# Layer 0's last tile of pairs made half as high and stacked, the split groups dealt out anew, two relus moved

## The chip, the core and the metric

The kernel runs on one core of a Trainium2 chip. The metric is the device time in microseconds (us) of one launch.

## What is computed

A batch of 512 rows looks up 39 embedding tables of width 16. A compressed interaction network of three layers follows, and then a small MLP. Cut to what matters (B = 512, 39 fields, D = 16):

```
x0 = xk = e                                    # (B, 39, 16), gathered
for idx, (W, b) in enumerate(params):          # three layers of 128 outputs
    z = relu(einsum('bhd,bkd,hks->bsd', x0, xk, W) + b[None, :, None])
    if idx != 2:
        xk = z[:, :64, :]; direct.append(z[:, 64:, :])
    else:
        direct.append(z)
h = concatenate([sum(concatenate(direct, axis=1), axis=-1), dense_ctx], axis=1)
y = relu(relu(h @ W_top1 + b_top1) @ W_top2 + b_top2) @ W_top3
```

## The kernel before

The batch is cut into C = 16 pieces of 32 rows, so that a row of a tile has N = 32 x 16 = 512 elements. A *tile* is a set of up to 128 pairs (a field of x0 and a row of xk), one on each partition. VectorE multiplies the two factors (`multiply`, L404), and TensorE contracts the tile with 128 x 128 weights into PSUM. Layers 1 and 2 have 39 x 64 pairs: 19 full tiles and one of 64 partitions (T1 = 20). Layer 0 is symmetric. Its 780 pairs lie in T0 = 7 full tiles, whose factors are `x0_same` (one anchor field for each partition, copied by the runs in `ANCHORS`) and `x0_rep` (the fields in rotation, `field_of`).

Tiles go in *groups* of two. `KINDS` gives each group a letter:

- `w`, whole: fp32 matmuls on the product as it is (L516, two instructions for a tile).
- `p` and `d`, split: ScalarE rounds the product (`round_high`, L625), GpSimd (`p`) or VectorE (`d`) subtracts to get the low part (`low_part`, L280), and TensorE makes three fp32r matmuls for each tile (L522, L524, L527).
- `h`, the last group of layers 1 and 2: one whole tile (L507), then the tile of 64 partitions, whose high and low parts lie one above the other in `stacks`. ScalarE makes the high part (L619), VectorE the low part (L423), and TensorE one fp32r matmul of 128 rows (L509) and one of 64 (L510).

```
KINDS = {1: "pwppwpwddh", 0: "dwww", 2: "wdwpwpwpwh"}
BODY = L1_GROUPS + L0_GROUPS + L2_GROUPS
```

A body for piece c walks through the 24 groups of BODY in order: indices 0 to 9 are layer 1 of piece c, 10 to 13 are layer 0 of piece c+1 and 14 to 23 are layer 2 of piece c. Layer 0 of piece 0 goes ahead of all bodies, and the last body has no layer 0. Every engine has its own instruction stream in this order, bound by semaphores:

- VectorE makes the products into a ring of 8 groups. The pairs (0, 1) and (2, 3) are one instruction each (`PAIRED`). The lows of its `d` and `h` groups come two groups late (`LOW_LAG`), and those still open are made at the latest ahead of layer 2. Index 0 waits for xk0, index 14 for xk1. xk0 and xk1 are PSUM banks; `x0_same` and `x0_rep` are in SBUF.
- ScalarE rounds, and it runs the relus that write xk and the direct outputs: layer 2 of the piece before at index 4, layer 1 at index 12, layer 0 of the next piece at index 18, each ahead of that index's rounding.
- GpSimd makes its lows in order. At index 10 it issues the ten indirect DMAs of `gather(c + 2)` (L360).
- SyncE's queue writes the gathered piece to DRAM (L297), loads `x0_same` with one DMA for each run of `ANCHORS` (L306), and then `x0_rep` in four parts of tiles, 0 to 3, 4 to 7, 8 to 13 and 14 to 19, two DMAs for each (L315).

Rounded and low parts have a ring of three slots (`PART_RING`). A slot is free when TensorE has used what was in it.

Of the kernel before, what the change touches and what calls it, by code (L numbers as in the profile page):

```python
# [41 lines left out]
def pairs_of_layer0():  # L42

    found = {}
    for t in range(T0):
        for p in range(S):
# [6 lines left out]
PARTS = [(0, 4), (4, 8), (8, 14), (14, T1)]  # L53


def part_of(t):

    return next(q for q, (first, end) in enumerate(PARTS) if first <= t < end)


# [10 lines left out]
STACKED = "whole, its second tile split and stacked"  # L71
LETTER = {"w": WHOLE, "d": LOW_DVE, "p": LOW_POOL, "h": STACKED}
# [20 lines left out]
SPLIT = [i for i, g in enumerate(BODY) if g[4] in (LOW_DVE, LOW_POOL)]  # L93
STACKS = [i for i, g in enumerate(BODY) if g[4] == STACKED]

RING = 8
# [12 lines left out]
    "split": lambda g: g[4] in (LOW_DVE, LOW_POOL),  # L109
    "stacked": lambda g: g[4] == STACKED,  # L110
    LOW_DVE: lambda g: g[4] == LOW_DVE,
# [37 lines left out]
def dlrm_cin_kernel(nc, ids, base, tables, dense, w0a, w0b, b0, bx0, w1, b1, bx1, w2, b2,  # L149
# [6 lines left out]
    with ctx:  # L156
# [130 lines left out]
        def _(sp):  # L287
# [20 lines left out]
            def load_replicated(c, half, q):  # L308

                first, end = PARTS[q]  # L310
                for e in range(2):
                    src = x0_rows[bass.ds(c, 1), T1 * e + first:T1 * e + first + 1, :]
# [14 lines left out]
            load_same(1, 1)  # L327
            sp.wait_ge(w_copied, len(BODY))
            sp.wait_ge(w_stack_made, len(STACKS))
# [57 lines left out]
        def _(dve):  # L387
# [31 lines left out]
            def make_low(c, index):  # L419
                if index in STACKS:  # L420
                    dve.wait_ge(stack_rounded, count("stacked", c, index))
                    at = STACKS.index(index)
                    nc.vector.tensor_tensor(stacks[HALF:128, at, :], products[0:HALF, index % RING, 1, :],  # L423
                                            stacks[0:HALF, at, :].bitcast(fp32), ALU.subtract).then_inc(stack_low, 1)
                else:
                    low_part(dve, nc.vector, c, index)

            def body(c, indices):
                late = []
                for index in indices:  # L430
                    layer, t, n, _, kind = BODY[index]
                    if layer == 1:
                        if t == 0:
                            dve.wait_ge(xk0_ready, c + 1)
                        if t == PARTS[part_of(t)][0]:
                            dve.wait_ge(rep_loaded[part_of(t)], 32 * (c + 1))
                    if layer == 0:
                        if t == 0:
                            dve.wait_ge(same_loaded, 16 * len(ANCHORS) * (c + 2))
                        if t == PARTS[part_of(t)][0]:  # L440
                            dve.wait_ge(rep_loaded[part_of(t)], 32 * (c + 2))
                    if layer == 2 and t == 0:
# [25 lines left out]
            for n_taken, index in enumerate(WEIGHT_ORDER):  # L468
# [5 lines left out]
                if index in WHOLES:  # L474
                    nc.vector.tensor_copy(w_whole[0:p, WHOLES.index(index), 0:n, :],
                                          w_sb[layer][0:p, t:t + n, :]).then_inc(w_copied, 1)
                else:
                    at = SPLIT.index(index)
# [5 lines left out]
            for at, index in enumerate(STACKS):  # L484
                layer, t = BODY[index][:2]
                dve.wait_ge(w_stack_rounded, at + 1)
                nc.vector.tensor_tensor(w_stack_low[:, at, :], w_sb[layer][0:HALF, t + 1, :],  # L487
                                        w_stack_high[0:HALF, at, :].bitcast(fp32), ALU.subtract) \
# [9 lines left out]
        def _(pe):  # L498
            tiles = [T0, T1, T1]

            def contract(c, index):
                layer, t, n, partitions, kind = BODY[index]
                slot, out = index % RING, z[layer][:, :]
                if kind == STACKED:
                    at, stack = WHOLES.index(index), STACKS.index(index)
                    pe.wait_ge(made, count("all", c, index))
                    nc.tensor.matmul(out, w_whole[:, at, 0, :], products[:, slot, 0, :], start=False, stop=False)  # L507
                    pe.wait_ge(stack_low, count("stacked", c, index))
                    nc.tensor.matmul(out, w_stack_high[:, stack, :], stacks[:, stack, :], start=False, stop=False)  # L509
                    mm = nc.tensor.matmul(out, w_stack_low[:, stack, :], stacks[0:HALF, stack, :],  # L510
                                          start=False, stop=True)
                elif kind == WHOLE:
                    at = WHOLES.index(index)
                    pe.wait_ge(made, count("all", c, index))
                    for i, p in enumerate(partitions):
                        mm = nc.tensor.matmul(out, w_whole[0:p, at, i, :], products[0:p, slot, i, :],  # L516
                                              start=(t + i == 0), stop=(t + i == tiles[layer] - 1))
                else:
                    at, part = SPLIT.index(index), part_slot(index)
                    pe.wait_ge(rounded, count("split", c, index))  # L520
                    for i, p in enumerate(partitions):
                        nc.tensor.matmul(out, w_high[0:p, at, i, :], high[0:p, part, i, :],  # L522
                                         start=(t + i == 0), stop=False)
                        nc.tensor.matmul(out, w_low[0:p, at, i, :], high[0:p, part, i, :], start=False, stop=False)  # L524
                    pe.wait_ge(low_by[kind], count(kind, c, index))
                    for i, p in enumerate(partitions):
                        mm = nc.tensor.matmul(out, w_high[0:p, at, i, :], low[0:p, part, i, :],  # L527
                                              start=False, stop=(t + i == tiles[layer] - 1))
                mm.then_inc(used, 1)

            def body(c, indices):
                first = isinstance(c, int) and c == 0
                for index in indices:
                    layer, t = BODY[index][:2]
                    if t == 0 and layer == 0 and not (isinstance(c, int) and c < 0):
                        pe.wait_ge(direct0_ready, c + 1)
                    if t == 0 and layer == 1 and not first:
                        pe.wait_ge(direct1_ready, c)
                    if t == 0 and layer == 2 and not first:
# [4 lines left out]
            pe.wait_ge(w_copied, len(BODY))  # L544
            pe.wait_ge(w_stack_made, len(STACKS))
# [49 lines left out]
        def _(act):  # L595
# [15 lines left out]
            def round_high(c, index):  # L611

                _, _, n, (p, *_), _ = BODY[index]
                if index in STACKS:
                    at = STACKS.index(index)
                    if not (isinstance(c, int) and c == 0):
                        act.wait_ge(used, count("all", c - 1, index))
                    act.wait_ge(made, count("all", c, index))
                    nc.scalar.activation(stacks[0:HALF, at, :], products[0:HALF, index % RING, 1, :],  # L619
                                         ACT.Copy).then_inc(stack_rounded, 1)  # L620
# [41 lines left out]
            for n_taken, index in enumerate(WEIGHT_ORDER):  # L662
# [7 lines left out]
                if index in STACKS:  # L670
                    nc.scalar.activation(w_stack_high[:, STACKS.index(index), :], w_sb[layer][:, t + 1, :],
                                         ACT.Copy).then_inc(w_stack_rounded, 1)
# [4 lines left out]
            for index in LAYER0:  # L677
                if index in SPLIT:
                    round_high(-1, index)
# [67 lines left out]
```

## Time and profile before

| | |
|---|---|
| median of 3 runs | 667.73 us (666.85 to 668.83) |
| the profiled execution | 668.06 us, its span 666.2 us |
| PE (TensorE matmul) busy | 625.0 us, 94% |
| DVE (VectorE) busy | 576.7 us, 87% |
| POOL (GpSimd) busy | 463.1 us, 70% |
| ACT (ScalarE) busy | 283.8 us, 43% |

In rows of the trace a name such as L404 is a line of the kernel. An instruction's duration can overlap the next one's on the same engine, so that the distance from start to start is what it costs its engine.

### The profile page before, as it was taken

How to read it: one execution, taken by the hardware profiler on the slowest of the kernel's cores; microseconds unless marked ns; L12 is line 12 of the kernel's file. 1: busy time of each engine (PE TensorE's matmuls, PEld its weight loads, DVE VectorE, ACT ScalarE, POOL GpSimd, SP SyncE). 2: the span in 40 equal slices, each digit the busy share in tenths (PEclk: the TensorE clock that was granted, in tenths of full speed). 3: DMA queues.
4: the chain of work that ended last, by engine and by line, in shares of the span. 5: the costliest groups of instructions: out<-in, count | busy, mean ns of one | idle time of the engine just before them, and what ended most of it. 6: DMA issues, size and time to landing. Idle time of an engine off the chain costs nothing.

```text
span 666.2 us, 7143 instructions
## 1 busy us (share of the span) xinstructions
PE 625.0 (94%) x1916; PEld 357.9 (54%) x1916; DVE 576.7 (87%) x507; ACT 283.8 (43%) x341; POOL 463.1 (70%) x277
## 2 busy tenths in 40 slices
PE   0358999999999999999999999999999999999998
PEld 0124555565555555555655555555655555555553
DVE  3139899999999999999999999999999999999670
ACT  3014444534454444444444444445444544445223
POOL 5607678686987878786978878786868878716340
PEclk9997999999999999999999999999999999999999
DMA  6698787694949495785939395876949395862000
GB/s 226 149 214 185 158 198 149 148 202 105 217 94 221 81 221 115 178 171 130 215 82 220 77 225 102 196 153 145 202 98 217 81 218 104 199 131 67 1 1 0
DMA packets 27422, 98.19 MB, mean 147 GB/s; under 512 B 7377, under 2 KB 16337, under 8 KB 18962
## 3 DMA queue, kind: packets, MB, share of 16 engines
q1 hardware_dynamic: 20930, 94.05, 63.9%
q0 software_dynamic: 5120, 1.32, 2.0%
q10 hardware_dynamic: 1360, 2.69, 1.1%
q14 instruction: 9, 0.07, 0.1%
q8 instruction: 3, 0.05, 0.0%
HBM read 94.20 MB, written 3.84 MB: 147 GB/s over the span
## 4 chain that ended last, share of the span: by engine, by line
PE 81%; DVE 6%; issue 3%; ACT 2%; POOL 1%; DVEq 0%; ACTq 0%; POOLq 0%
PE z L516 37%; PE z L527 12%; PE z L522 12%; PE z L524 11%; DVE products L404 5%; PE z L507 4%; PE z L510 2%; POOL low L280 1%; PE z L509 1%; PE spare L560 1%; ACT high L625 1%; PE z L584 1%; DVE low L280 1%; PE xk L584 1%; ACT xk L609 0%
## 5 line engine op out<-in xcount | busy, mean ns | idle before, releaser
L404 DVE TENSOR_TENSOR products<-x_rep,xk 128x1024 f32<-128x1024 f32 (+1 forms) x288 | 366.7, 1333 | 29.1 <-ACT xk L609 19.8
L280 POOL TENSOR_TENSOR low<-products,high 128x1024 fp32r<-128x1024 f32 x112 | 264.9, 2390 | 131.5 <-ACT high L625 90.0
L516 PE MATMUL z<-products,w_whole 128*128 128x512 f32 x672 | 312.9, 598 | 0.0
L625 ACT ACTIVATE high<-products 128x1024 fp32r<-128x1024 f32 x176 | 184.3, 1056 | 242.1 <-DVE products L404 200.1
L360 POOL DMA_INDIRECT gathered<-in_tables,rows_sb x160 | 197.5, 1234 | 46.5 <-issue 44.6
L522 PE MATMUL z<-high,w_high 128*128 128x512 f32 x352 | 188.0, 534 | 15.8 <-ACT high L625 15.8
L516 PEld LDWEIGHTS z<-products,w_whole 128*128 128x128 f32 x672 | 128.5, 191 | 112.8 <-issue 98.0
L524 PE MATMUL z<-high,w_low 128*128 128x512 f32 x352 | 139.7, 397 | 0.0
L527 PE MATMUL z<-low,w_high 128*128 128x512 f32 x352 | 113.9, 404 | 3.7 <-DVE low L280 2.9
L522 PEld LDWEIGHTS z<-high,w_high 128*128 128x128 f32 x352 | 66.9, 190 | 61.6 <-issue 33.2
L280 DVE TENSOR_TENSOR low<-products,high 128x1024 fp32r<-128x1024 f32 x64 | 93.8, 1467 | 1.3 <-ACT high L625 1.3
L524 PEld LDWEIGHTS z<-high,w_low 128*128 128x128 f32 x352 | 67.0, 190 | 36.0 <-issue 26.8
L404 DVE TENSOR_TENSOR products<-x_rep,x_same 128x1024 f32 (+1 forms) x64 | 69.3, 1084 | 17.1 <-DMA x_rep<-x_rows 16.6
L527 PEld LDWEIGHTS z<-low,w_high 128*128 128x128 f32 x352 | 64.0, 189 | 29.6 <-POOL low L280 13.1
L609 ACT ACTIVATE xk<-z,bx_sb 64x512 f32<-64x512 f32 x64 | 41.7, 651 | 85.7 <-PE z L510 72.2
L423 DVE TENSOR_TENSOR stacks<-products,stacks 64x512 fp32r<-64x512 f32 x32 | 31.7, 992 | 11.9 <-ACT stacks L619 11.3
L609 ACT ACTIVATE direct<-z,b_sb 64x512 f32<-64x512 f32 (+1 forms) x48 | 32.5, 678 | 15.4 <-PE z L510 8.1
L507 PE MATMUL z<-products,w_whole 128*128 128x512 f32 x64 | 32.6, 591 | 0.0
L619 ACT ACTIVATE stacks<-products 64x512 fp32r<-64x512 f32 x32 | 19.9, 622 | 19.2 <-DVE products L404 19.2
L509 PE MATMUL z<-stacks,w_stack_high 128*128 128x512 f32 x32 | 25.4, 792 | 0.0
L549 PE MATMUL spare<-products 16*128 16x512 f32 x6 | 5.5, 1078 | 19.0 <-DVE w_stack_low L487 19.0
L415 DVE TENSOR_REDUCE logit<-direct 128x512 f32 (+1 forms) x16 | 10.9, 679 | 7.6 <-ACT direct L609 7.6
(34 smaller groups left out, 102.5 us busy)
## 6 DMA issues: line engine op xcount, KB each, us to landing
x_rep<-x_rows SPq DMA_DIRECT2D x64, 768.0 KB, 16.7
x_rep<-x_rows SPq DMA_DIRECT2D x64, 512.0 KB, 9.3
x_rows<-gathered SPq DMA_DIRECT2D x16, 225.0 KB
x_rep<-in_w ACTq DMA_DIRECT2D x2, 1280.0 KB, 9.9
gathered<-in_tables,rows_sb POOLq DMA_INDIRECT x160
x_same<-x_rows SPq DMA_DIRECT2D x16, 90.0 KB
x_same<-x_rows SPq DMA_DIRECT2D x16, 78.0 KB
x_rep<-in_wt SPq DMA_DIRECT2D x2, 512.0 KB, 4.0
```

What stands on the lines that cost most here:

```text
L280: ops.tensor_tensor(low[0:p, slot, 0:n, :], products[0:p, index % RING, 0:n, :], high[0:p, slot, 0:n, :].bitcast(fp32), ALU.subtract).then ...
L360: pool.indirect_dma_start(out=gathered[:, c % 2, j * D:(j + 1) * D], out_offset=None, in_=tables, in_offset=bass.IndirectOffsetOnAxis(ap=r ...
L404: nc.vector.tensor_tensor(slots, rep, row.unsqueeze(1).broadcast_to([p, n, N]), ALU.mult).then_inc(made, 1 + pair)
L423: nc.vector.tensor_tensor(stacks[HALF:128, at, :], products[0:HALF, index % RING, 1, :], stacks[0:HALF, at, :].bitcast(fp32), ALU.subtract ...
L507: nc.tensor.matmul(out, w_whole[:, at, 0, :], products[:, slot, 0, :], start=False, stop=False)
L509: nc.tensor.matmul(out, w_stack_high[:, stack, :], stacks[:, stack, :], start=False, stop=False)
L516: mm = nc.tensor.matmul(out, w_whole[0:p, at, i, :], products[0:p, slot, i, :], start=(t + i == 0), stop=(t + i == tiles[layer] - 1))
L522: nc.tensor.matmul(out, w_high[0:p, at, i, :], high[0:p, part, i, :], start=(t + i == 0), stop=False)
L524: nc.tensor.matmul(out, w_low[0:p, at, i, :], high[0:p, part, i, :], start=False, stop=False)
L527: mm = nc.tensor.matmul(out, w_high[0:p, at, i, :], low[0:p, part, i, :], start=False, stop=(t + i == tiles[layer] - 1))
L609: return nc.scalar.activation(out, in_, RELU, bias=bias)
L625: nc.scalar.activation(high[0:p, slot, 0:n, :], products[0:p, index % RING, 0:n, :], ACT.Copy).then_inc(rounded, 1)
```

## The change

Layer 0's 780 pairs are laid out with six runs of anchors in place of four, so that they fit in six full tiles and one of 64 partitions. The upper half of `x0_rep` holds its tiles in a turned order (`row_of`). The tile of 64 partitions is a group of its own (`s`, ALONE), split and stacked as in `h` but with no whole tile, and it stands third in layer 0. The letters of all layers are dealt anew: in layer 1 `p` stands at 1, 2 and 4 (before: 0, 2, 3 and 5), and in layer 2 at 16, 18, 20 and 22 (before: 17, 19 and 21, with a `d` at 15). In layer 0 `d` stands at 11 and 13 (before: 10). Whole tiles in a body fall from 23 to 22, split tiles stay at 22, stacks rise from 2 to 3. ScalarE runs layer 1's relus at index 14 and layer 0's at 19; VectorE's sum over layer 2's output moves from index 8 to 6.

```
-ANCHORS = [(0, F, 0), (F, HALF - F, F - 2 * T0), (HALF, 19, 6), (HALF + 19, 45, 32)]
+TURNED = 5
+ANCHORS = [(0, 34, 12), (34, 30, 14), (HALF, 9, 5), (73, 6, 6), (79, F, 1), (118, 10, 31)]
+def row_of(e, t):
+    return T1 + (t + TURNED) % (T1 - 1) if e else t
 def field_of(p, t):
-    return (p % HALF + p // HALF * T1 + t) % F
+    return (p % HALF + row_of(p // HALF, t)) % F
...
-KINDS = {1: "pwppwpwddh", 0: "dwww", 2: "wdwpwpwpwh"}
+KINDS = {1: "wppwpwwddh", 0: "wdsd", 2: "wwpwpwpwph"}
 def groups_of(layer, tiles, partitions):
     found, t = [], 0
     for letter in KINDS[layer]:
+        if letter == "s":
+            found.append((layer, tiles - 1, 1, partitions[-1:], ALONE))
+            tiles -= 1
+            continue
...
-L0_GROUPS = groups_of(0, T0, [S] * T0)
+L0_GROUPS = groups_of(0, T0, [S] * (T0 - 1) + [HALF])
-STACKS = [i for i, g in enumerate(BODY) if g[4] == STACKED]
+STACKS = [i for i, g in enumerate(BODY) if g[4] in (STACKED, ALONE)]
...                                  # VectorE
-                    if kind in (LOW_DVE, STACKED):
+                    if kind in (LOW_DVE, STACKED, ALONE):
                         late.append(index)
-                    if index == 8 and not (isinstance(c, int) and c == 0):
+                    if index == 6 and not (isinstance(c, int) and c == 0):
                         logits2(c - 1)
...                                  # TensorE
-                if kind == STACKED:
-                    at, stack = WHOLES.index(index), STACKS.index(index)
-                    pe.wait_ge(made, count("all", c, index))
-                    nc.tensor.matmul(out, w_whole[:, at, 0, :], products[:, slot, 0, :], start=False, stop=False)
+                if kind in (STACKED, ALONE):
+                    stack = STACKS.index(index)
+                    if kind == STACKED:
+                        pe.wait_ge(made, count("all", c, index))
+                        nc.tensor.matmul(out, w_whole[:, WHOLES.index(index), 0, :], products[:, slot, 0, :],
+                                         start=False, stop=False)
                     pe.wait_ge(stack_low, count("stacked", c, index))
...                                  # ScalarE
-                    if index == N1 + 2:
+                    if index == N1 + 4:
                         after_layer1(c)
-                    if index == N1 + N0 + 4 and not last:
+                    if index == N1 + N0 + 5 and not last:
                         after_layer0(c)
```

## Rows read from the trace of the kernel before

**Rows 1.** Waits from 80 to 600 us: total us, times, longest us.

```profile
DVE products L404 <- ACT xk L609: 11.5, 14, 0.8
PEld z L527 <- POOL low L280: 11.0, 28, 0.6
```

**Rows 2.** Timeline of TensorE in one body: start us, us, engine, line, operation.

```profile
507.68 0.73 PE L527 MATMUL z<-low,w_high 128*128 128x512 f32 x2
508.25 1.88 PE L516 MATMUL z<-products,w_whole 128*128 128x512 f32 x4
...
511.35 1.88 PE L516 MATMUL z<-products,w_whole 128*128 128x512 f32 x4
...
515.84 1.02 PE L507 MATMUL z<-products,w_whole 128*128 128x512 f32 x2
...
517.01 0.49 PE L510 MATMUL z<-stacks,w_stack_low 64*128 64x512 f32 x1
...
517.77 0.40 PE L524 MATMUL z<-high,w_low 128*128 128x512 f32 x1
...
518.93 6.17 PE L516 MATMUL z<-products,w_whole 128*128 128x512 f32 x14
...
525.16 0.39 PE L524 MATMUL z<-high,w_low 128*128 128x512 f32 x1
```

**Rows 3.** Timeline of VectorE, from index 14 to the next index 14.

```profile
481.85 4.62 DVE L404 TENSOR_TENSOR products<-x_rep,xk 128x1024 f32<-128x1024 f32 x4 [0.81 <-ACT xk L609]
...
495.68 1.28 DVE L423 TENSOR_TENSOR stacks<-products,stacks 64x512 fp32r<-64x512 f32 x1 [0.70 <-ACT stacks L619]
496.99 10.14 DVE L404 TENSOR_TENSOR products<-x_rep,xk 128x2048 f32<-128x2048 f32 x7
...
508.77 2.27 DVE L280 TENSOR_TENSOR low<-products,high 128x1024 fp32r<-128x1024 f32 x1
510.96 1.21 DVE L404 TENSOR_TENSOR products<-x_rep,x_same 128x1024 f32 x1
...
514.48 0.69 DVE L423 TENSOR_TENSOR stacks<-products,stacks 64x512 fp32r<-64x512 f32 x1
...
518.98 4.62 DVE L404 TENSOR_TENSOR products<-x_rep,xk 128x1024 f32<-128x1024 f32 x4 [0.82 <-ACT xk L609]
```

**Rows 4.** Timeline of ScalarE in the same body: rounding of index 17.

```profile
486.50 1.06 ACT L625 ACTIVATE high<-products 128x1024 fp32r<-128x1024 f32 x1 [1.21 <-DVE products L404]
```

**Rows 5.** Timeline of GpSimd in the same body.

```profile
491.69 4.72 POOL L280 TENSOR_TENSOR low<-products,high 128x1024 fp32r<-128x1024 f32 x2 [0.86 <-ACT high L625]
500.51 9.45 POOL L280 TENSOR_TENSOR low<-products,high 128x1024 fp32r<-128x1024 f32 x4 [4.10 <-PE z L516]
510.11 1.77 POOL L360 DMA_INDIRECT gathered<-in_tables,rows_sb  x1
512.18 1.95 POOL L360 DMA_INDIRECT gathered<-in_tables,rows_sb  x1 [0.30 <-issue]
...
524.27 1.27 POOL L360 DMA_INDIRECT gathered<-in_tables,rows_sb  x1 [0.30 <-issue]
```

**Rows 6.** The group of relus to xk, whole span: busy us, mean ns, idle before.

```profile
L609 ACT ACTIVATE xk<-z,bx_sb 64x512 f32<-64x512 f32 x64 | 41.7, 651 | 85.7 <-PE z L510 72.2 <-PE z L516 12.7
```

**Rows 7.** Timeline of SyncE's queue, body 0, loading piece 1.

```profile
51.99 1.31 SPq L306 DMA_DIRECT2D x_same<-x_rows  x4
53.40 5.27 SPq L315 DMA_DIRECT2D x_rep<-x_rows  x8
```

**Rows 8.** Tile x_rep on SyncE's queue: the second DMA of tiles 4 to 7.

```profile
L315 SPq DMA_DIRECT2D x_rep<-x_rows x1: 597/597/597, 55.2 to 55.2; - x1
...
DMA to landing us min/median/max: 12.3/12.3/12.3
```

**Rows 9.** Timeline of VectorE in body 0.

```profile
67.64 1.22 DVE L404 TENSOR_TENSOR products<-x_rep,x_same 128x1024 f32<-128x1024 f32 x1
...
72.92 1.22 DVE L404 TENSOR_TENSOR products<-x_rep,xk 128x1024 f32<-128x1024 f32 x1 [2.32 <-ACT xk L609]
```

More of the change, by code:

```diff
@@ L45, in pairs_of_layer0 @@
     for t in range(T0):
-        for p in range(S):
+        for p in range(S if t < T0 - 1 else HALF):
             pair = frozenset((anchor_of(p), field_of(p, t)))
@@ L53, with parts_new @@
 PARTS = [(0, 4), (4, 8), (8, 14), (14, T1)]
+assert all(row_of(1, end - 1) - row_of(1, first) == end - 1 - first for first, end in PARTS)
 def part_of(t):
     return next(q for q, (first, end) in enumerate(PARTS) if first <= t < end)
+def parts_new(index):
+    layer, t, n = BODY[index][:3]
+    tiles = range(t, t + n)
+    before = {part_of(u) for i in range(STARTS[layer], index) for u in range(BODY[i][1], BODY[i][1] + BODY[i][2])}
+    return sorted({part_of(u) for u in tiles} - before)
 DENSE = 16
@@ L71 @@
 STACKED = "whole, its second tile split and stacked"
-LETTER = {"w": WHOLE, "d": LOW_DVE, "p": LOW_POOL, "h": STACKED}
-KINDS = {1: "pwppwpwddh", 0: "dwww", 2: "wdwpwpwpwh"}
+ALONE = "one tile of 64 partitions, split and stacked"
+LETTER = {"w": WHOLE, "d": LOW_DVE, "p": LOW_POOL, "h": STACKED, "s": ALONE}
+KINDS = {1: "wppwpwwddh", 0: "wdsd", 2: "wwpwpwpwph"}
 def groups_of(layer, tiles, partitions):
@@ L422, in make_low @@
                     at = STACKS.index(index)
-                    nc.vector.tensor_tensor(stacks[HALF:128, at, :], products[0:HALF, index % RING, 1, :],
+                    nc.vector.tensor_tensor(stacks[HALF:128, at, :], products[0:HALF, index % RING, BODY[index][2] - 1, :],
                                             stacks[0:HALF, at, :].bitcast(fp32), ALU.subtract).then_inc(stack_low, 1)
@@ L476, in _ @@
                                           w_sb[layer][0:p, t:t + n, :]).then_inc(w_copied, 1)
-                else:
+                elif index in SPLIT:
                     at = SPLIT.index(index)
@@ L486, in _ @@
                 dve.wait_ge(w_stack_rounded, at + 1)
-                nc.vector.tensor_tensor(w_stack_low[:, at, :], w_sb[layer][0:HALF, t + 1, :],
+                nc.vector.tensor_tensor(w_stack_low[:, at, :], w_sb[layer][0:HALF, t + BODY[index][2] - 1, :],
                                         w_stack_high[0:HALF, at, :].bitcast(fp32), ALU.subtract) \
@@ L498, in _ @@
         def _(pe):
-            tiles = [T0, T1, T1]
             def contract(c, index):
@@ L503, in contract @@
                 slot, out = index % RING, z[layer][:, :]
-                if kind == STACKED:
-                    at, stack = WHOLES.index(index), STACKS.index(index)
-                    pe.wait_ge(made, count("all", c, index))
-                    nc.tensor.matmul(out, w_whole[:, at, 0, :], products[:, slot, 0, :], start=False, stop=False)
+                first, last = index == STARTS[layer], index == ENDS[layer]
+                if kind in (STACKED, ALONE):
[4 more added lines that the diff above has]
+                                         start=False, stop=False)
                     pe.wait_ge(stack_low, count("stacked", c, index))
-                    nc.tensor.matmul(out, w_stack_high[:, stack, :], stacks[:, stack, :], start=False, stop=False)
+                    nc.tensor.matmul(out, w_stack_high[:, stack, :], stacks[:, stack, :], start=first, stop=False)
                     mm = nc.tensor.matmul(out, w_stack_low[:, stack, :], stacks[0:HALF, stack, :],
-                                          start=False, stop=True)
+                                          start=False, stop=last)
                 elif kind == WHOLE:
@@ L516, in contract @@
                         mm = nc.tensor.matmul(out, w_whole[0:p, at, i, :], products[0:p, slot, i, :],
-                                              start=(t + i == 0), stop=(t + i == tiles[layer] - 1))
+                                              start=(first and i == 0), stop=(last and i == n - 1))
                 else:
@@ L522, in contract @@
                         nc.tensor.matmul(out, w_high[0:p, at, i, :], high[0:p, part, i, :],
-                                         start=(t + i == 0), stop=False)
+                                         start=(first and i == 0), stop=False)
                         nc.tensor.matmul(out, w_low[0:p, at, i, :], high[0:p, part, i, :], start=False, stop=False)
@@ L527, in contract @@
                         mm = nc.tensor.matmul(out, w_high[0:p, at, i, :], low[0:p, part, i, :],
-                                              start=False, stop=(t + i == tiles[layer] - 1))
+                                              start=False, stop=(last and i == n - 1))
                 mm.then_inc(used, 1)
@@ L533, in body @@
                 for index in indices:
-                    layer, t = BODY[index][:2]
-                    if t == 0 and layer == 0 and not (isinstance(c, int) and c < 0):
+                    if index == STARTS[0] and not (isinstance(c, int) and c < 0):
                         pe.wait_ge(direct0_ready, c + 1)
-                    if t == 0 and layer == 1 and not first:
+                    if index == STARTS[1] and not first:
                         pe.wait_ge(direct1_ready, c)
-                    if t == 0 and layer == 2 and not first:
+                    if index == STARTS[2] and not first:
                         pe.wait_ge(direct2_ready, c)
@@ L615, in round_high @@
                     at = STACKS.index(index)
-                    if not (isinstance(c, int) and c == 0):
+                    if not (isinstance(c, int) and c == (-1 if index in LAYER0 else 0)):
                         act.wait_ge(used, count("all", c - 1, index))
                     act.wait_ge(made, count("all", c, index))
-                    nc.scalar.activation(stacks[0:HALF, at, :], products[0:HALF, index % RING, 1, :],
+                    nc.scalar.activation(stacks[0:HALF, at, :], products[0:HALF, index % RING, n - 1, :],
                                          ACT.Copy).then_inc(stack_rounded, 1)
@@ L670, in _ @@
                 if index in STACKS:
-                    nc.scalar.activation(w_stack_high[:, STACKS.index(index), :], w_sb[layer][:, t + 1, :],
+                    nc.scalar.activation(w_stack_high[:, STACKS.index(index), :], w_sb[layer][:, t + n - 1, :],
                                          ACT.Copy).then_inc(w_stack_rounded, 1)
@@ L677, in _ @@
             for index in LAYER0:
-                if index in SPLIT:
+                if index in SPLIT + STACKS:
                     round_high(-1, index)
```

28 lines of the change are left out of this document (16 added, 12 removed).

## The prediction

> **What bounds the kernel now.** I read the page's busy shares first: TensorE is at 94%, but VectorE at 87% is close enough to ask which of them paces a body. The waits answer that in part [rows 1]. Between 80 and 600 us VectorE waits once in each of 14 bodies, about 0.82 us, for xk1 at index 14. TensorE's weight loads wait some 11 us in 28 waits, two in a body, for GpSimd's lows. So the two hold each other up in a ring, and the timelines show its links.
>
> Let X be the start of index 14 on VectorE and P the start of the pair (0, 1). VectorE goes from X = 481.85 to P = 496.99 in 15.14 us, and from there to the next X = 518.98 in 21.99, of which 0.82 is the wait: work to P+21.17 [rows 3]. A body is 37.13. What ends the wait? GpSimd starts its first low at P+3.52 and makes four at 2.36 each [rows 5]; TensorE takes up the third at 507.68, P+10.69, and from there needs 9.82 to the end of layer 1 (517.01 + 0.49 = P+20.51) [rows 2]. Two relus of 0.65 follow [rows 6], and index 14 starts 1.48 after layer 1's end. The sum is 10.69 + 9.82 + 1.48 + 15.14 = 37.13, the body.
>
> TensorE's prices [rows 2]: a half of a whole tile costs (525.16 - 0.23 - 518.93) / 14 = 0.43, so a tile 0.86 and a group of two 1.72. From 508.25 to 511.35 is a whole group and a split one, so the split one costs 1.38 (0.23 for each fp32r matmul). The stack: 515.84 + 0.86 = 516.70 is its start, and the second matmul of the group behind it starts at 517.77. That is 1.07 less one matmul of 0.23, or 0.84 for two matmuls that should cost 0.46. By the sum of its tiles (23 whole, 22 split, 2 stacks) a body needs 36.64, and 0.4 to 0.5 is stall.
>
> **A wait to see before the sum.** VectorE's subtractions for low parts read two operands in SBUF. The one at 508.77 takes 2.27 against 1.21 for a plain one, and the next product starts 2.19 later. GpSimd's fourth low ends at 500.51 + 9.45 = 509.96, and 509.96 + 1.07 = 511.03 is just the end of VectorE's. The stack at 495.68 takes 1.28 against 0.69 at 514.48, and ends 0.55 after GpSimd's low ends (491.69 + 4.72 = 496.41) [rows 3, 5]. So a subtraction that meets a running low waits for its end and then runs in full; products from xk, which is in PSUM, show nothing of the kind.
>
> **The change, part by part.**
>
> *TensorE.* One whole tile (0.86) becomes a stack (0.84): a body needs 36.62, nothing gained. Bounds: nothing, or 0.40 if the stack cost only its matmuls; I take nothing, because the stack measured has the same neighbour, a split group.
>
> *First half, P to X.* VectorE's products keep their number and sizes. At index 7's low GpSimd has only three lows in layer 1 behind it, which end at P + 3.52 + 2x2.36 + 2.38 = P+10.62; the low starts at P+11.78 and is no longer held: -1.06. Added in this half are the stack of index 12 (0.71, as from low 9 to the next product) and a second `d` in layer 0, which is 1.13 moved here from index 15. Work now ends at 21.17 - 1.06 + 0.71 + 1.13 = P+21.95. Index 13's rounding is ready in time (product at P+17.75, rounded by P+20.1, wanted at P+20.8). ScalarE turns to layer 1's relus only after it, at P+20.1, behind which wait the direct output and all of layer 2's rounding. TensorE's first hold-up in layer 1 is now the second low, ready at P+8.26; from there it has 9.82 plus one more whole group, so layer 1 ends at P+20.0. xk1 then comes at about P+21.4 and its reader could go at P+21.5. The wait of 0.82 is gone, but VectorE's own work is later than what it waited for: X = P+21.95.
>
> *Second half, X to P.* The low of 15 is gone (-1.13), so VectorE comes to the stack of 23 at X + 13.83 - 1.13 = X+12.70. But layer 2 now has GpSimd's low at 22, directly ahead of it. Its time comes from ScalarE. Products start 1.13 apart and a rounding starts 1.25 after its product's start [rows 3, 4], so that of 18 is X+5.78 to 6.84. Now layer 0's three relus stand behind it (0.66 + 0.66 + 0.68), and 20 is rounded from X+8.9 to 9.95. GpSimd makes 20 from X+10.09 and 22 from X+12.44 to 14.82. The stack at X+12.70 meets it, waits, and ends at 15.37: P = X+15.40, against 15.14. The loop's own overhead, 1.3 us behind the stack, stays hidden under that wait.
>
> A body is then 21.95 + 15.40 = 37.35, against 37.13: +0.2 in 14 bodies, +3.1 us (a careful reading of the pitches, good to 0.15 a body, leaves 1 to 5). TensorE absorbs 0.7 us of stall.
>
> *Gather.* It starts at P+10.75 instead of P+13.12. Alone an issue takes 1.25; the ten here take 15.43 instead of 12.2, and the long ones lie under layer 0's products and lows [rows 5], which are two-operand work: 3.2 us over 8.2 us of it. There are now 10.2 us of it, so 4.0 us more than alone: the gather ends near P+26.9, X+5.0, against X+4.7 at which the first low of layer 2 could start. That 0.3 is lost again ahead of low 20, which waits for ScalarE until X+10.09. Bounds: nothing extra, or 5.5 us (X+6.5), which is the third rival.
>
> *Relu and sum moves.* Layer 2's sum at index 6 starts at P+7.8; its relu is done by P+6.3, so nothing. Layer 0's relus are costed above.
>
> *The start.* Layer 0 of piece 0 would end 2 to 3 us sooner: one `w` goes ahead of the `d`, and less of the work is whole. It is not kept. Piece 1's tiles 4 to 7 land at 55.2 + 12.3 = 67.5 [rows 8], and VectorE reads them at 67.64 [rows 9]. That landing cannot come sooner. Two more `x0_same` DMAs at 0.33 each [rows 7] stand ahead of it for piece 0, whose loads fill the queue, and again for piece 1: +1.3, so 68.8. From there to index 14 is 0.6 + 1.13 + 1.2 + 0.71 + 1.13 = 4.8: X = 73.6 against 72.92, and P a further 0.26 later: +1.0. Bounds: 0 and +1.5. In later bodies the parts land 8 us or more before use.
>
> *The end.* The last body has no layer 0 and TensorE's layer 1 ends at P+20.0 instead of 20.5: -0.6. Layer 2 has 15.8 us of TensorE work in either kernel.
>
> Sum: +3.1 + 1.0 - 0.6 = +3.5 by the profiled execution (668.06, 0.33 above the median). My rounding in each link errs to the long side by a few hundredths (ScalarE starts a rounding that is already waiting 0.95 after the last, not 1.06), so I take +2.8: **670.5 us**.
>
> **Rivals.** *The stack goes first.* The margin at X+12.70 is 0.26 us: if GpSimd's low of 22 is not yet running, VectorE takes the stack at once, reaches P by X+14.0 (the loop's overhead), and its body is 35.95. TensorE is then the bound at 36.7 to 36.9 (its xk1 link). For it: the margin is small. Against: both times hang on X alone, in every body alike. It decides as soon as low 22 starts 0.26 later. Time: 14 x -0.35 + 1.0 - 0.6 = -4.5, 663 us (661.5 at the best). The Trainium skill (SBUF — State Buffer, "Who interferes with whom") says that whichever of the two engines issues first gets the shared port and the other fully blocks; by that GpSimd's low would then be the one to wait, about 0.7 us, which layer 2's TensorE work covers.
>
> *VectorE's first half is shorter than summed.* If index 14 could start with xk1 at P+21.5 and the second half loses nothing, the body is 36.9 to 37.15. For it: it takes 0.3 us of overestimate in 37. Against: the same prices give the old body to 0.01. Time 665.5 to 668, no change that shows.
>
> *GpSimd becomes the bound.* If the gather ends at X+6.5, four lows follow (9.45), and the stack behind them: P = X + 6.5 + 9.45 + 0.58 = X+16.5. A body of 38.5 gives 686. It decides from X+5.4 on, and an end at X+5.7 gives 37.7 and 673 to 675. For it: GpSimd has 33 us of work in a ring of 37. Against: it begins the gather 2.4 us sooner. By a page of the Trainium skill (SBUF — State Buffer, the same section) a two-input tensor_tensor takes only the pair's read side while descriptors need the write side, which it calls inferred; by that the gather would not be slowed at all and this rival would have no chance. The 3.2 us that the rows show speak otherwise.
>
> **How the numbers follow.** No change from before can be told within 0.3%, 665.7 to 669.7. Forecast (668.5 to 673): 0.48. Stack first: 0.17. Shorter half: 0.20. GpSimd bound: 0.15. The forecast's lower third lies within 0.3%. Faster: the stack-first case and a little of the third, 0.22. Same: 0.30. Slower: 0.48. The range of 662.5 to 675 leaves out 0.05 below and about 0.1 above.
>
> **What would show it.** The stack of index 23 ends about 0.55 after a low of GpSimd, with a duration near 2.7; index 7's low takes 1.2; VectorE's wait for xk1 shrinks to under 0.1; TensorE's waits for lows grow to 0.6 or more a body, in layer 1's third group; 14 stands 37.3 from 14; VectorE waits for `x0_rep` near 68 us. A stack of 23 with 0.69 us and bodies under 37 make me wrong, as does a stack in layer 0 that costs 0.5 on TensorE in a body where TensorE is the bound.

## The result: 1.2% slower

The changed kernel takes 676.23 us (median of 4 runs) against 668.19 (also 4), a ratio of 1.0119 (95% interval 1.0102 to 1.0136). That is the way that was forecast, and 1.2 us beyond the end of the range. The profiled execution took 677.12 us with a span of 675.3, 9.1 more than before.

The page of the changed kernel: busy time by engine, then the chain that ended last, by engine and by line.

```profile
PE 627.4 (93%) x1916; PEld 357.3 (53%) x1916; DVE 600.2 (89%) x523; ACT 294.4 (44%) x358; POOL 485.6 (72%) x277
...
POOL 47%; PE 23%; issue 14%; DVE 7%; DMA 5%; ACT 3%; SPq 1%; DVEq 1%; POOLq 0%; ACTq 0%
POOL gathered L384 30%; POOL low L304 17%; PE z L541 11%; DVE products L428 6%; PE z L552 4%; ACT high L649 2%; PE z L547 2%; PE z L549 2%; DMA x_rows<-gathered 2%; DMA x_rep<-x_rows 2%; DMA gathered<-in_tables,rows_sb 2%; PE spare L584 1%; PE z L608 1%; PE xk L608 1%; PE z L531 1%
```

In the kernel before, the same line of the page gave TensorE 81% of the chain and GpSimd 1%. Now GpSimd has 47%, and 30% is the gather's DMA issues alone. Busy shares (94% to 93% for TensorE, 70% to 72% for GpSimd) show none of this.

The timeline of VectorE in one body of the changed kernel, from P = 503.52 to the next P = 541.42:

```profile
503.52 7.88 DVE L428 TENSOR_TENSOR products<-x_rep,xk 128x2048 f32<-128x2048 f32 x5
...
515.30 1.22 DVE L304 TENSOR_TENSOR low<-products,high 128x1024 fp32r<-128x1024 f32 x1
...
520.67 1.82 DVE L428 TENSOR_TENSOR products<-x_rep,x_same 64x512 f32 x2
522.42 1.21 DVE L304 TENSOR_TENSOR low<-products,high 128x1024 fp32r<-128x1024 f32 x1
523.66 0.69 DVE L447 TENSOR_TENSOR stacks<-products,stacks 64x512 fp32r<-64x512 f32 x1
524.38 1.23 DVE L304 TENSOR_TENSOR low<-products,high 128x1024 fp32r<-128x1024 f32 x1
525.52 5.74 DVE L428 TENSOR_TENSOR products<-x_rep,xk 128x1024 f32<-128x1024 f32 x5
...
538.20 3.19 DVE L447 TENSOR_TENSOR stacks<-products,stacks 64x512 fp32r<-64x512 f32 x1 [0.70 <-ACT stacks L643]
541.42 2.29 DVE L428 TENSOR_TENSOR products<-x_rep,xk 128x2048 f32<-128x2048 f32 x1
```

P is again the start of the pair (0, 1) on VectorE and X that of index 14, here 525.52. Set it beside [rows 3]. The first half, P to X, is 22.00 us (summed: 21.95), with no wait for xk1 left. The low of index 7 takes 1.22, not 2.27. The second half is 15.90 (summed: 15.40; before 15.14), and its last instruction, the stack of index 23, takes 3.19 us. A body is 37.90.

The timeline of GpSimd in the same body:

```profile
507.04 7.09 POOL L304 TENSOR_TENSOR low<-products,high 128x1024 fp32r<-128x1024 f32 x3 [4.11 <-ACT high L649]
514.27 0.96 POOL L384 DMA_INDIRECT gathered<-in_tables,rows_sb  x1
515.53 1.80 POOL L384 DMA_INDIRECT gathered<-in_tables,rows_sb  x1 [0.30 <-issue]
517.64 1.97 POOL L384 DMA_INDIRECT gathered<-in_tables,rows_sb  x1 [0.30 <-issue]
519.91 0.95 POOL L384 DMA_INDIRECT gathered<-in_tables,rows_sb  x1 [0.30 <-issue]
521.16 3.29 POOL L384 DMA_INDIRECT gathered<-in_tables,rows_sb  x1 [0.30 <-issue]
524.75 1.67 POOL L384 DMA_INDIRECT gathered<-in_tables,rows_sb  x1 [0.30 <-issue]
526.73 0.94 POOL L384 DMA_INDIRECT gathered<-in_tables,rows_sb  x1 [0.30 <-issue]
...
530.46 0.95 POOL L384 DMA_INDIRECT gathered<-in_tables,rows_sb  x1 [0.30 <-issue]
531.43 9.41 POOL L304 TENSOR_TENSOR low<-products,high 128x1024 fp32r<-128x1024 f32 x4
```

An issue takes 0.95 when it is let alone, and up to 3.29 while VectorE makes layer 0's products and lows. The ten end at 531.41, P+27.89, X+5.89, and the four lows of layer 2 start at once, back to back. The fourth ends at 531.43 + 9.41 = 540.84, and the stack, which waits for it, at 541.39. So the ring, the closed chain of waits that sets the length of a body, is now: pair (0, 1), first rounding, three lows, the gather, four lows, the stack, pair (0, 1):

3.52 + 7.09 + 0.14 + 17.14 + 0.02 + 9.41 + 0.58 = 37.90.

But for the pauses of 0.30 between issues, the only idle time of GpSimd is the 4.11 us ahead of the first low. TensorE needs 36.6 in a body and stalls for the rest: 0.35 at the second low of layer 1 and 0.88 at the first low of layer 2, which the gather has held up.

**Where the 9.1 us are.** Between the first P inside the loop and the P of the last body lie 14 bodies: 530.10 us (86.57 to 616.67) against 520.38 (88.13 to 608.51), +9.7. The start gives back 1.6 and the end takes 0.9.

### The profile page after: what moved, and what is told of

The parts are those of the page before. It is cut to its first block, busy times and chain, and to the rows that moved or that the text cites. A ratio compares the mean times of both kernels' runs of the same rounds, so it can differ in the third digit from the quotient of the medians.

```text
span 675.3 us, 7235 instructions
## 1 busy us (share of the span) xinstructions
PE 627.4 (93%) x1916; PEld 357.3 (53%) x1916; DVE 600.2 (89%) x523; ACT 294.4 (44%) x358; POOL 485.6 (72%) x277
## 4 chain that ended last, share of the span: by engine, by line
POOL 47%; PE 23%; issue 14%; DVE 7%; DMA 5%; ACT 3%; SPq 1%; DVEq 1%; POOLq 0%; ACTq 0%
POOL gathered L384 30%; POOL low L304 17%; PE z L541 11%; DVE products L428 6%; PE z L552 4%; ACT high L649 2%; PE z L547 2%; PE z L549 2%; DMA x_rows<-gathered 2%; DMA x_rep<-x_rows 2%; DMA gathered<-in_tables,rows_sb 2%; PE spare L584 1%; PE z L608 1%; PE xk L608 1%; PE z L531 1%
## 5 line engine op out<-in xcount | busy, mean ns | idle before, releaser
L541 PE MATMUL z<-products,w_whole 128*128 128x512 f32 x640 | 302.5, 603 | 13.4 <-DVE products L428 13.4
L384 POOL DMA_INDIRECT gathered<-in_tables,rows_sb x160 | 220.8, 1380 | 46.5 <-issue 44.8
L547 PE MATMUL z<-high,w_high 128*128 128x512 f32 x352 | 193.3, 549 | 0.0
L541 PEld LDWEIGHTS z<-products,w_whole 128*128 128x128 f32 x640 | 119.5, 191 | 124.6 <-issue 100.8
L552 PE MATMUL z<-low,w_high 128*128 128x512 f32 x352 | 113.2, 403 | 12.9 <-POOL low L304 10.2
L428 DVE TENSOR_TENSOR products<-x_rep,x_same 128x1024 f32 (+3 forms) x64 | 68.0, 1083 | 19.6 <-DMA x_rep<-x_rows 17.2
L447 DVE TENSOR_TENSOR stacks<-products,stacks 64x512 fp32r<-64x512 f32 x48 | 71.0, 1480 | 12.3 <-ACT stacks L643 11.3
L304 DVE TENSOR_TENSOR low<-products,high 128x1024 fp32r<-128x1024 f32 x64 | 77.9, 1218 | 0.5
L643 ACT ACTIVATE stacks<-products 64x512 fp32r<-64x512 f32 x48 | 30.3, 631 | 10.4 <-DVE products L428 8.3
L531 PE MATMUL z<-products,w_whole 128*128 128x512 f32 x64 | 32.7, 591 | 0.0
L534 PE MATMUL z<-stacks,w_stack_high 128*128 128x512 f32 x48 | 32.2, 670 | 0.0
L535 PE MATMUL z<-stacks,w_stack_low 64*128 64x512 f32 x48 | 24.1, 502 | 0.0
```

What stands on the lines that cost most here:

```text
L304: ops.tensor_tensor(low[0:p, slot, 0:n, :], products[0:p, index % RING, 0:n, :], high[0:p, slot, 0:n, :].bitcast(fp32), ALU.subtract).then ...
L384: pool.indirect_dma_start(out=gathered[:, c % 2, j * D:(j + 1) * D], out_offset=None, in_=tables, in_offset=bass.IndirectOffsetOnAxis(ap=r ...
L428: nc.vector.tensor_tensor(slots, rep, row.unsqueeze(1).broadcast_to([p, n, N]), ALU.mult).then_inc(made, 1 + pair)
L531: nc.tensor.matmul(out, w_whole[:, WHOLES.index(index), 0, :], products[:, slot, 0, :], start=False, stop=False)
```

## The experiments

Each run is compared with the kernel before, by medians of 667.4 to 667.9 from 9 to 19 launches of it. "A body" is the mean distance from P to P over twelve bodies of the loop; before it is 37.17, after the change 37.90.

### Which part of the ring sets the body

*p21: layer 2's lows one group earlier.*

```
-KINDS = {1: "wppwpwwddh", 0: "wdsd", 2: "wwpwpwpwph"}
+KINDS = {1: "wppwpwwddh", 0: "wdsd", 2: "wpwpwpwpwh"}
```

> The changed kernel with layer 2's GpSimd letters one group earlier (15, 17, 19, 21 in place of 16, 18, 20, 22), so that a whole group stands between the last low and the stack of 23. Theory A (a ring through GpSimd: three lows, the slowed gather, four lows, then the stack of 23 that the last low holds up, then the pair (0, 1)): the four lows still start when the gather ends, so the last one ends where it did; a body stays at 37.9, within 0.1, and TensorE's stall moves to layer 2's second group, 2 us. Theory B (the low directly ahead of the stack is the cause, as in the prediction's sum): the stack is free about 1.1 us sooner and a body falls to 36.8 to 37.1, 12 us less in all.

Measured: 674.98 us, ratio 1.0110 (1.0084 to 1.0137), a body of 37.90. The last low started at P+34.95 in both kernels, though its group now stands one place further from the stack. So the lows go when the gather lets them, and theory B, on which my own sum rested, is out for this kernel.

*gather3: three of ten issues moved into GpSimd's idle time.*

```
-            def gather(c):
+            def gather(c, columns=range(GB)):
...
-                for j in range(GB):
+                for j in columns:
...
-                    if index == N1 and c + 2 < C:
-                        gather(c + 2)
+                    if index == 0 and c + 2 < C:
+                        gather(c + 2, range(3))
+                    if index == N1 and c + 2 < C:
+                        gather(c + 2, range(3, GB))
```

> The changed kernel with three of the ten gathers issued at index 0, where GpSimd idles 4.1 us in every body, and seven at index 10. Theory A: the gather at index 10 ends some 3.8 us or more sooner, GpSimd leaves the ring, and what the prediction summed is left: low 22 then starts after ScalarE's rounding, X+12.4, the stack ends at X+15.4, a body is 37.35, 8 us less in all. Theory B: 0.5 us of a body is something else than the gather, and a body stays at 37.9. Theory C, the rival of the free port: low 22 starts so that the stack goes first, a body of 36.7.

Measured: 669.14 us, ratio 1.0019 (1.0005 to 1.0032), a body of 37.28. One of its ten launches took 3590 us and is left out of the ratio; why is open. With the gather out of the ring, what is left is the forecast's body of 37.35, to 0.07. The timeline of its GpSimd in layer 2 has the break that the forecast described, low 20 waiting for ScalarE:

```profile
523.33 4.72 POOL L304 TENSOR_TENSOR low<-products,high 128x1024 fp32r<-128x1024 f32 x2 [2.56 <-ACT high L651]
528.58 4.73 POOL L304 TENSOR_TENSOR low<-products,high 128x1024 fp32r<-128x1024 f32 x2 [0.54 <-ACT high L651]
```

*both: the two edits together.*

> The two edits together: letters at 15, 17, 19, 21, and three gathers at index 0. Theory A: with the gather out of the ring the last low (21) can start at X+11.3 and end at X+13.7, the stack ends at X+14.3, VectorE's body is 36.3, and TensorE is the bound: 36.7 to 36.8, about 16 us less than the changed kernel, some 8 less than the kernel before (660). If only the letters matter, the same as p21; if only the gather, the same as gather3.

Measured: 658.75 us, ratio 0.9869 (0.9848 to 0.9890), a body of 36.61; TensorE's tiles add up to 36.62. The letters, worth nothing alone, are worth 0.67 us a body once the gather is out of the way.

*before_gather3: the same move of three issues in the kernel before (same diff).*

> The kernel before, with three of its ten gathers issued at index 0. A control: in the kernel before GpSimd is free again before layer 2's first low is ready, so by theory A the gather is in no ring there and a body stays at 37.1 to 37.2. If shorter gathers help any such kernel (less traffic under the products, an earlier load of the next piece), it gains as gather3 did, 0.6 a body, 9 us in all.

Measured: 667.95 us, ratio 0.9995 (0.9983 to 1.0007), a body of 37.17. The gather is in no ring there. The expectation was wrong in one point: GpSimd is not free before layer 2's first low is ready. In the kernel before the gather ends at P+28.55 and this low starts right behind it, at P+28.57; with the move it starts at P+27.84. But the next low waits for ScalarE and starts at P+31.8 in both, so nothing is gained.

### Why the gather got longer

*l0_psum: layer 0's products with one operand in PSUM.*

```
...                                  # VectorE, products of layer 0
                     row = x0_same[0:p, bass.ds(half, 1), :].rearrange("p a n -> p (a n)")
+                    if not (isinstance(c, int) and c == -1):
+                        row = xk[0][0:p, :]
```

> The changed kernel, but layer 0's products of all bodies read xk of layer 1 (PSUM) in place of x0_same (SBUF) as their second operand, which leaves out part of the computation: layer 0 of pieces 1 to 15 multiplies by the wrong factor. Nothing else moves. Theory A: these four products no longer slow the gather; it falls from 17.2 to about 15 us, and a body from 37.9 to 37.35 to 37.4. If the gather is slowed by VectorE being busy at all, and not by its second SBUF operand, the gather stays at 17.2 and a body at 37.9.

Measured: 667.70 us, ratio 1.0002 (0.9989 to 1.0015), a body of 37.27, and the ten issues take 15.89 us in place of 17.14. The same instructions at the same places, with one operand in another memory, slow the gather by 1.25 us less. The fifth issue falls from 3.29 us to 0.94; the next two then meet later lows and grow from 1.67 to 2.03 and from 0.94 to 1.67 (the timeline of its GpSimd):

```profile
512.80 0.94 POOL L384 DMA_INDIRECT gathered<-in_tables,rows_sb  x1 [0.30 <-issue]
514.05 0.94 POOL L384 DMA_INDIRECT gathered<-in_tables,rows_sb  x1 [0.30 <-issue]
515.30 2.03 POOL L384 DMA_INDIRECT gathered<-in_tables,rows_sb  x1 [0.30 <-issue]
517.63 1.67 POOL L384 DMA_INDIRECT gathered<-in_tables,rows_sb  x1 [0.30 <-issue]
```

The gather still takes 3.7 us over its 12.2, under the low parts, which read two SBUF operands yet. That they cause all of it was not tried.

*l0_whole: layer 0's small tile whole and last, no third stack.*

```
-KINDS = {1: "wppwpwwddh", 0: "wdsd", 2: "wwpwpwpwph"}
+KINDS = {1: "wppwpwwddh", 0: "wddw", 2: "wwpwpwpwph"}
```

> The changed kernel with layer 0's tile of 64 partitions whole and last (wddw), not split and stacked. VectorE loses the stack's low (0.71) and that much two-operand work. Theory A: the gather takes about 16.8 in place of 17.1, the ring through GpSimd is 37.5 to 37.6, 4 to 5 us less than the changed kernel. If the stack were what costs, the body would fall by its full VectorE price, to 37.2.

Measured: 664.43 us, ratio 0.9956 (0.9938 to 0.9974), a body of 37.06. More than I gave it: the issues take 16.28 us, 0.86 less, though VectorE's two-operand work fell by 0.71. The ring still closes through GpSimd: gather's end at P+27.05, four lows (9.41), the stack (0.59) = 37.05. But TensorE is level with it. In the later bodies it waits for no low, its whole tile of 64 rows costs 0.38 more than the stack did (both_whole, below), and it catches up by only 0.02 us a body (X comes that much sooner after P each time). Its own body is thus 37.04, and a still shorter gather could have given hardly more. This version leaves out layer 0's stack, and with it moves the second `d` from index 13 to 12. It is faster than the kernel before, so the stack cost the changed kernel its loss, by way of the gather.

### The letters and the relus

*before_letters: the kernel before with the new letters of layers 1 and 2 only.*

```
-KINDS = {1: "pwppwpwddh", 0: "dwww", 2: "wdwpwpwpwh"}
+KINDS = {1: "wppwpwwddh", 0: "dwww", 2: "wwpwpwpwph"}
...
-                    if index == N1 + N0 + 4 and not last:
+                    if index == N1 + N0 + 5 and not last:
```

> The kernel before (layer 0 in seven full tiles, dwww) with only the new letters of layers 1 and 2, and layer 0's relus at index 19. Theory A: VectorE comes to layer 2 some 1.9 us sooner in its body, the two-operand work under the gather is 8.3 us as before, the gather takes 15.4 and ends at X+4.7, ScalarE's chain and not the gather sets the last low, and VectorE's body is 36.9; TensorE needs 36.98 (25 whole tiles, 20 split, 2 stacks). A body is 37.0 to 37.1: no loss. If the new place of GpSimd's lows is harmful by itself, a body is 37.9 here too.

Measured: 673.57 us, ratio 1.0091 (1.0073 to 1.0109), a body of 37.67: neither theory's number. The gather did as expected (15.44 us, ending at X+4.85, and low 20 waits for ScalarE). The loss is in the first half, P+22.39 in place of the prediction's P+21.5 for xk1, and ScalarE's waits tell why:

```profile
ACT high L625 <- PE z L527: 84.0, 14, 6.1
```

With `dwww` there are ten split groups, not eleven, and the ring of three part slots turns otherwise: index 1 now gets the slot of index 22, and its rounding waits, in each of 14 bodies, until TensorE is through with 22. The first low starts at P+4.59, not 3.52. I had not counted the slots. The run clears the gather and says nothing clean on the letters.

*old_letters: the changed kernel with the old letters of layers 1 and 2.*

```
-KINDS = {1: "wppwpwwddh", 0: "wdsd", 2: "wwpwpwpwph"}
+KINDS = {1: "pwppwpwddh", 0: "wdsd", 2: "wdwpwpwpwh"}
```

> The changed kernel (layer 0 as wdsd, relus at 14 and 19) with the old letters of layers 1 and 2: four lows ahead of the gather, three behind it, one more low for VectorE. TensorE would need only 36.3. Theory A: the gather starts at P+13.1 and takes 17.1; three lows follow (7.1) and the stack (0.6), so the ring through GpSimd is 3.52 + 9.45 + 0.13 + 17.1 + 7.1 + 0.6 = 37.9; VectorE's first half has its held-up low again (P+23.0). A body of 37.9 to 38.1. If the letters of layers 1 and 2 caused the loss, a body falls under 37.2.

Measured: 686.05 us, ratio 1.0276 (1.0259 to 1.0293), a body of 38.52. The ring is the one described and closes, but the gather takes 17.75, not 17.1, as the low of index 15 falls on its ninth issue (1.61 us): lows to P+12.97, gather from P+13.11 to 30.86, three lows (7.05), the stack (0.60). Under layer 0's new form the new letters save 0.6 us a body.

*relu_early: layer 1's relus back at index 12.*

```
-                    if index == N1 + 4:
+                    if index == N1 + 2:
```

> The changed kernel with layer 1's relus back at index 12. ScalarE then waits for TensorE's end of layer 1 (P+19.85) before it rounds the stack of 12 and the group 13, whose lows VectorE makes ahead of layer 2: the stack's low at P+22.6, the low of 13 at P+23.7, X = P+24.9 in place of 22.0. By theory A the gather's end at P+27.9 is then X+3.0 and out of the ring, and P' = X+15.4: a body of 40.2, some 32 us more than the changed kernel. If the place of the relus does not matter, 37.9.

Measured: 706.50 us, ratio 1.0574 (1.0542 to 1.0607), a body of 39.97. The stack's low of index 12 starts at P+22.61, after a wait of 2.50, the next product at P+24.70. The move of this relu is a condition of the rest. That of layer 0's was not tried by itself.

### What a stack costs TensorE

*before_pad: the kernel before with the stack's second matmul at full height, 64 rows of zero weights added.*

```
-w_stack_low = sb("w_stack_low", [HALF, len(STACKS), S], fp32r)
+w_stack_low = sb("w_stack_low", [128, len(STACKS), S], fp32r)
...                                  # at the start, beside the lower half
+                upper = w_sb[layer][HALF:128, t + 1, :]
+                nc.vector.tensor_tensor(w_stack_low[HALF:128, at, :], upper, upper, ALU.subtract) \
+                    .then_inc(w_stack_made, 1)
...                                  # TensorE
-                    mm = nc.tensor.matmul(out, w_stack_low[:, stack, :], stacks[0:HALF, stack, :],
+                    mm = nc.tensor.matmul(out, w_stack_low[:, stack, :], stacks[:, stack, :],
```

> The kernel before, with the stack's second matmul made as high as its neighbours: its weights get 64 more rows, all zero, and it reads all 128 partitions of the stack. The result is the same. Theory A says that the stack's 0.84 is 0.46 of matmuls and 0.38 of changing from 128 rows to 64 and back; without the change of height layer 1 ends 0.38 sooner, xk1 too, and the ring of the kernel before is 36.75: -0.38 a body, 5 to 6 us less. If the extra time belongs to the stack's data and not to the height, 37.15 as before.

Measured: 664.46 us, ratio 0.9956 (0.9939 to 0.9973), a body of 36.99. The timeline of its TensorE around the stack:

```profile
513.30 1.02 PE L510 MATMUL z<-products,w_whole 128*128 128x512 f32 x2
513.75 0.80 PE L512 MATMUL z<-stacks,w_stack_high 128*128 128x512 f32 x1
514.39 0.40 PE L513 MATMUL z<-stacks,w_stack_low 128*128 128x512 f32 x1
514.63 0.40 PE L525 MATMUL z<-high,w_high 128*128 128x512 f32 x1
514.86 0.39 PE L527 MATMUL z<-high,w_low 128*128 128x512 f32 x1
```

Read as in [rows 2], the stack costs 514.86 - 514.16 - 0.23 = 0.47 in place of 0.84, so the price of the height is there. But the body fell by 0.18, half of what I expected, and the half can be named. From the stack's start to the end of layer 1 it was 0.80 (516.70 to 517.50) and is 0.63 (514.16 to 514.79), so about 0.18 lay ahead of layer 1's end. The other 0.20 lay behind it, in the next group's first two matmuls. Only the first part is in the ring that ends at xk1. X moved from P+21.99 to P+21.80.

*both_pad: both edits and the padded weights.*

> The version with both edits (letters one earlier, three gathers at index 0) and the padded stack weights. TensorE then needs 36.62 - 3 x 0.38 = 35.5 and is no longer the bound; VectorE's own body (P+22.0, then 14.2 to the next pair) is: 36.2, some 6 us less than both: 652 to 653. If heights cost nothing, 36.6 again.

Measured: **651.59 us, ratio 0.9757 (0.9741 to 0.9774)**, a body of 36.16 from the third body on (the second took 37.44). This is the fastest of all the versions, 2.4% under the kernel before. The timeline of its TensorE around a stack:

```profile
503.18 1.02 PE L536 MATMUL z<-products,w_whole 128*128 128x512 f32 x2
503.63 0.80 PE L539 MATMUL z<-stacks,w_stack_high 128*128 128x512 f32 x1
504.27 0.40 PE L540 MATMUL z<-stacks,w_stack_low 128*128 128x512 f32 x1
504.50 1.02 PE L546 MATMUL z<-products,w_whole 128*128 128x512 f32 x2
```

From 503.18 + 0.86 = 504.04 to 504.50 the stack costs 0.46, against 0.84 in [rows 2]. VectorE is now the bound, as expected: X is at P+22.00 and the next P 14.16 behind it.

*both_whole: both edits, and layer 0 as in l0_whole.*

> The version with both edits, with wddw in layer 0: TensorE is the bound there, so this weighs the stack against a whole tile of 64 rows. By the heights' price the whole tile costs 0.86 and about 0.4 for its change of height, against 0.86 for the stack: a body of 36.9 to 37.0 against 36.6. If heights cost nothing it is 36.6.

Measured: 663.60 us, ratio 0.9933 (0.9912 to 0.9953), a body of 37.07 but for the first two of the loop. A lone tile of 64 rows pays for the change of height whether it is split or not. TensorE's starts show 1.25 us for the whole tile (517.53 to 518.78) against 0.87 for the stack, 0.38 more; the steady body grew by 0.43, from 36.64 to 37.07, and the rest of that is open.

## Why the forecast had the sign and not the size

**Right, by its own steps.** TensorE gained nothing: layer 0's stack costs 0.87 (from 526.50, where it starts, to the second matmul behind it at 527.60, less 0.23; summed 0.84). The first half is 22.00 (21.95), TensorE's hold-up in layer 1 is at the second low, and the stack of 23 ends 0.55 after the low that it met. The stall at that second low was to be 0.6 us or more; it is 0.35 in the changed kernel and 0.6 in gather3, where nothing else holds TensorE. gather3 shows the sum itself: without the gather in the ring a body is 37.28, and the forecast said 37.35. But that mechanism is worth 0.11 us a body over the 37.17 before, and it does not set the changed kernel's body (p21). Of the 0.73 measured the rest is the gather's, so the direction came out right mainly for a reason to which the forecast had given a chance of 0.15.

**The step that failed** is the gather: "so 4.0 us more than alone: the gather ends near P+26.9, X+5.0 ... That 0.3 is lost again ahead of low 20". That the gather is slowed was right, the size was not: it is 4.9 us more than alone and it ends at X+5.89, behind the X+5.4 from which the ring closes through GpSimd. (And nothing was lost again ahead of low 20: two lows from there end at X+10.6, later than ScalarE's X+10.09.) I had taken one rate, 3.2 us of delay for 8.2 us of two-operand work. The third rival named this case, put its threshold at X+5.4 and its price at 37.7 us a body for X+5.7, and got a chance of 0.15. It is what happened: 37.90. The time that it gave for this, 673 to 675, is too short by its own terms: 14 x 0.57 + 1.0 - 0.6 on 668.06 is 676. The range ended at that 675. Its threshold was 0.4 us from the forecast's end, and the unknown had been bounded at 0 and 5.5 us, with 4.0 taken. A term whose threshold lies within its own bounds, so near the value taken, deserved more than that, a third by my estimate. The 10.2 us of two-operand work were as summed (515.30 to 525.52); the delay is not proportional to it: the instructions that start between 520.67 and 524.38 held up one issue, that of 521.16, by 2.3 us (3.29 against 0.95).

**The page that spoke against it.** The Trainium skill (SBUF — State Buffer, "Who interferes with whom") reports a probe in which tensor_tensor did not stall a DMA of this kind, and infers as the reason that it takes only the read side of the shared port pair while descriptor generation needs the write side. l0_psum decides against that here: issues that run under layer 0's products take 1.25 us less in all when the products' second operand is in PSUM.

**Two smaller misses.** The start was to cost 1.0 us and gave back 1.6. Tiles 4 to 7 of piece 1 landed 10.3 us after an issue at 56.0, at 66.3, and not 1.3 later than before but 1.2 sooner; "that landing cannot come sooner" treated a measured landing as a bound. What shortened it is open. The end was to give 0.6 and took 0.9. From the last P to the first matmul behind the logits it did give 0.6 (45.97 us against 46.59). The rest is the clock: in the last 15 us of the changed kernel TensorE's mean granted clock was 0.89, a part of the stretch at 1.2 GHz, the lower of its two levels, against 1.00 (2.4 GHz throughout) before, and the first four matmuls behind the logits took 3.4 us (662.64 to 666.00) in place of 1.8 (655.10 to 656.92):

```profile
660.00:675.00 15.00, 12.55 (x36) 5.60 (x36) 0.69 (x1) 5.06 (x8) 0.00 (x0) 0.89 0.00 0
```

In both kernels TensorE had waited for the logits and done their small matmuls just before. The profiled executions of gather3, l0_psum, l0_whole, both_whole and relu_early have these four at 3.1 to 3.4 us too; those of p21, both, both_pad and old_letters, and of all four versions with the old layer 0, have them at 1.8. So 1.5 of the 9.1 us are the clock's; whether the change has a part in that is open.

One term of the working was off without effect: layer 1's end, put at P+20.0, is P+19.8 by its own terms and was P+19.85.

**The rival of the free port** did not occur: in gather3, where it would have, low 22 started at P+34.30, 0.37 ahead of the stack.

## What to carry to other kernels

Write the ring of every engine that takes part, not only of those with a high share: GpSimd was busy 72% and had 33.8 us of chained work in a body of 37.9. A buffer ring shared by a list of members (here split groups modulo three slots) is part of the schedule, so count it anew whenever the list changes length. Where an engine idles at one point of the ring and is late at another, move independent work into the gap; that, layer 2's letters one group earlier and full-height stacks turned a loss of 1.2% into a gain of 2.4%. When a fix stops paying, ask what is level with it: in l0_whole TensorE was within 0.02 us a body of the ring through GpSimd.

## What the hardware showed unexpectedly

- Ten indirect DMA issues of GpSimd take 12.2 us alone (the ten of piece 1, ahead of the loop: 18.46 to 30.71 in the kernel before), 15.4 in the loop of the kernel before, 17.1 in the changed one, 17.8 in old_letters. A single one took 3.29 in place of 0.94.
- A matmul of 64 rows between matmuls of 128 costs about 0.38 us more than one of full height with zeros, 0.18 ahead of its end and 0.20 behind it (before_pad against the kernel before).
- A VectorE subtraction of two SBUF operands that starts while GpSimd makes a low waits for its end: 3.19 us for an instruction of 0.69, in the changed kernel's stack of index 23.
